# Norms behind the second feed-forward layer: the inverse deviations by GpSimd as a power, in place of ScalarE's square root and VectorE's reciprocal

## The reference, cut to what matters

```
h  = gelu(bi @ ffn_w1 + ffn_b1)
h  = gelu(h @ ffn_w2 + ffn_b2)
s  = x + h
H  = H + (s - mean(s)) * rsqrt(var(s) + 1e-5) * ln2_w + ln2_b
X  = (H - mean(H)) / sqrt(var(H) + 1e-5)
# then: per-channel and global extremes of X, from them scales and limits of an
# 8-bit quantization, quantized X and weights, a product, gelu, ...
```

## Time and profile before

| | us |
|---|---|
| median of three runs | 735.29 |
| lowest and highest of them | 730.75 and 736.48 |
| the profiled execution, its own time | 732.9 |
| its span in the profile | 730.9 |

### The profile page before, as it was taken

The page is one execution under the profiler, slowest core; times in us unless marked ns, Lnnn a source line. Parts: engine busy times, 40 slices in busy tenths (PEclk is TensorE's granted clock), DMA queues, the critical chain, the costliest instruction groups (busy, mean ns, idle before and its releaser), DMA issues.

```text
span 730.9 us, 13424 instructions
## 1 busy us (share of the span) xinstructions
PE 633.8 (87%) x4912; PEld 566.1 (77%) x4912; DVE 490.0 (67%) x1269; ACT 383.2 (52%) x875; POOL 277.1 (38%) x292
## 2 busy tenths in 40 slices
PE   3759898899899556568999999989999999999993
PEld 3659775569898432357888888979999999999993
DVE  3668688674604877657777785488587768677761
ACT  1349876873433466455665643442255656556540
POOL 5340525344301415042323353001244756666633
PEclk9959999999999756679999999999999999999997
DMA  6600000215000580300000110103095876768733
GB/s 181 120 1 5 1 1 1 98 50 147 1 0 1 148 150 0 120 0 5 4 4 4 25 72 2 48 1 120 19 320 153 250 234 198 261 177 254 200 95 69
DMA packets 27585, 64.67 MB, mean 88 GB/s; under 512 B 5951, under 2 KB 19152, under 8 KB 25184
## 3 DMA queue, kind: packets, MB, share of 16 engines
q0 software_dynamic: 12640, 46.90, 21.8%
q1 hardware_dynamic: 13116, 16.04, 8.3%
q10 hardware_dynamic: 1764, 0.88, 0.5%
HBM read 58.55 MB, written 5.74 MB: 88 GB/s over the span
## 4 chain that ended last, share of the span: by engine, by line
PE 46%; DVE 6%; issue 2%; ACT 2%; POOL 1%; DMA 0%; POOLq 0%; DVEq 0%; ACTq 0%
PE bank L1949 11%; PE bank L1909 4%; PE bank L1912 4%; PE bank L1913 4%; PE bank L1910 4%; PE bank L1911 4%; PE bank L1818 2%; PE bank L1754 2%; PE bank L1797 2%; DVE amx L2559 1%; PE bank L1774 1%; PE bank L1804 1%; PE bank L1716 1%; PE bank L1780 1%; DVE big L2565 1%
## 5 line engine op out<-in xcount | busy, mean ns | idle before, releaser
L2655 DVE TENSOR_SCALAR big<-bank 128x256 f32<-128x256 f32 (+1 forms) x126 | 52.3, 415 | 52.9 <-PE bank L1913 52.6
L1328 ACT ACTIVATE big<-bank 128x256 f32<-128x256 f32 (+1 forms) x126 | 47.5, 379 | 48.9 <-PE bank L1913 48.9
L811 POOL TENSOR_TENSOR big<-big,arc 128x423 f32<-128x423 f32 (+1 forms) x48 | 37.8, 814 | 73.6 <-DVE arc L2579 73.6
L837 POOL DMA_INDIRECT total<-big,goal x32 | 54.1, 1692 | 23.9 <-issue 17.5
L1909 PE MATMUL bank<-x_lead,w_lead 128*128 128x256 f32 x192 | 56.4, 294 | 0.0
L1912 PE MATMUL bank<-x_both,w_lead 128*128 128x256 f32 x192 | 54.4, 283 | 0.0
L1913 PE MATMUL bank<-x_both,w_rest 128*128 128x256 f32 x192 | 54.1, 282 | 0.0
L1911 PE MATMUL bank<-x_lead,w_rest 128*128 128x256 f32 x192 | 54.1, 282 | 0.0
L1910 PE MATMUL bank<-x_rest,w_lead 128*128 128x256 f32 x192 | 54.0, 281 | 0.0
L2666 DVE SCALAR_TENSOR_TENSOR big<-big 128x256 f32<-128x256 f32 (+1 forms) x126 | 50.4, 412 | 0.0
L844 POOL DMA_INDIRECT big<-x_rows,origin x32 | 34.0, 1061 | 33.9 <-DVE goal L2712 20.1
(11 more groups left out here) (542 smaller groups left out, 2022.9 us busy)
## 6 DMA issues: line engine op xcount, KB each, us to landing
big<-in_patches SPq DMA_DIRECT2D x2, 768.0 KB, 8.6
areg<-in_e_gate_up SPq DMA_DIRECT2D x1, 1536.0 KB, 6.5
shared_lead<-in_e_gate_up POOLq DMA_DIRECT2D x1, 1536.0 KB, 7.2
wreg<-in_ffn_w SPq DMA_DIRECT2D x1, 1152.0 KB
ffw_lead<-in_ffn_w POOLq DMA_DIRECT2D x1, 1152.0 KB, 7.8
out<-total SPq DMA_DIRECT2D x2, 423.0 KB
wreg<-in_in_w SPq DMA_DIRECT2D x2, 419.0 KB
wreg<-in_in_w SPq DMA_DIRECT2D x4, 209.5 KB
```

The costliest lines, as they stand in the source:

```text
L811: pool.tensor_tensor(o, o, arc[0:r, 18 * (b % 2) + 3 * g:18 * (b % 2) + 3 * g + q].unsqueeze(2).to_broadcast([r, q, L]), ALU.mult).then_in ...
L837: pool.indirect_dma_start(out=total, in_=YS[:, j % 2, q * D:(q + 1) * D], in_offset=None, out_offset=bass.IndirectOffsetOnAxis(ap=goal[:, ...
L1328: nc.scalar.activation(GS[:, n % 3, 0:w], bank[2 * (n % 2)][:, 0:w], ACT.Silu).then_inc(S["g_silu"], 1)
L2655: v.tensor_scalar(UM[:, n % 3, 0:w], bank[2 * (n % 2) + 1][:, 0:w], 10.0, -10.0, ALU.min, ALU.max).then_inc(S["u_clip"], 1)
```

## The change

GpSimd now computes, for each group, both inverse deviations: it adds 1e-5 to three variances (a `tensor_scalar` of 128x3), waits for that, and raises the sum to the power -0.5 (a `tensor_tensor` with a broadcast constant, operation `pow`). The first result goes to `rstd` as before, the second to `rstd2`. ScalarE's six square roots of this stage and VectorE's six reciprocals are gone. On VectorE the wait for the first inverse deviation moves behind the multiplication by the scale, in front of the instruction that reads it. On ScalarE the three `tokens_out` now stand behind all nine GELUs. The constant -0.5 is written once, while GpSimd has nothing else to do.

```diff
+            st.add(pool.memset(cst[:, 3:4], -0.5))
...
-            for t in range(6):
-                if t % 3 == 0:
-                    pool.wait_ge(S["rstd_ready"], t // 3 + 1)
-                pool.tensor_scalar(X[:, t, :], H[:, t, :], mv[:, t, 0:1], rstd[:, t:t + 1], ALU.subtract, ALU.mult).then_inc(ln_x, 1)
+            for g in range(3):
+                w = slice(3 * g, 3 * (g + 1))
+                pool.wait_ge(S["ln2_var"], 3 * (g + 1))
+                st.add(pool.tensor_scalar(std[:, w], mv[:, w, 1], EPS, None, ALU.add))
+                st.wait()
+                pool.tensor_tensor(rstd[:, w], std[:, w], cst[:, 3:4].to_broadcast([P, 3]), ALU.pow).then_inc(S["ln2_std"], 1)
+                pool.wait_ge(ln_var, TT + 3 * (g + 1))
+                st.add(pool.tensor_scalar(std[:, w], mv[:, w, 1], EPS, None, ALU.add))
+                st.wait()
+                pool.tensor_tensor(rstd2[:, w], std[:, w], cst[:, 3:4].to_broadcast([P, 3]), ALU.pow).then_inc(S["rstd_ready"], 1)
+                if g < 2:
+                    pool.wait_ge(S["rstd_ready"], g + 1)
+                    for t in range(3 * g, 3 * (g + 1)):
+                        pool.tensor_scalar(X[:, t, :], H[:, t, :], mv[:, t, 0:1], rstd2[:, t:t + 1], ALU.subtract, ALU.mult).then_inc(ln_x, 1)
...
             for t in range(TT):
                 act.wait_ge(S["f2_ready"], t + 1)
                 nc.scalar.activation(G2[0:rows(t), t, :], bank[4 + t % 4][0:rows(t), 0:D], ACT.Gelu).then_inc(S["f2_out"], 1)
-                if t % 3 == 2:
-                    deviations(t // 3, S["ln2_var"], t + 1, S["ln2_std"])
-                    if t == 5:
-                        tokens_out(0)
-                    if t == TT - 1:
-                        tokens_out(1)
-                    deviations(t // 3, ln_var, TT + t + 1, ln_std)
-            tokens_out(2)
+            for g in range(3):
+                tokens_out(g)
...
-                dve.wait_ge(ln_var, k * TT + 3 * (g + 1))
-                dve.wait_ge(ln_std, STD_BASE[k] + g + 1)
-                v.reciprocal(rstd[:, 3 * g:3 * (g + 1)], std[:, 3 * g:3 * (g + 1)]).then_inc(S["rstd_ready"], 1)
                 if g == 2:
...
-                dve.wait_ge(S["ln2_std"], g + 1)
-                st.add(v.reciprocal(rstd[:, 3 * g:3 * (g + 1)], std[:, 3 * g:3 * (g + 1)]))
                 for t in tiles3:
                     st.add(v.scalar_tensor_tensor(out=SS[:, t, :], in0=SS[:, t, :], scalar=mv[:, t, 0:1], in1=ln2w[:, :],
                                                   op0=ALU.subtract, op1=ALU.mult))
                 st.wait()
                 dve.wait_ge(S["x_kept"], TT + 1)
+                dve.wait_ge(S["ln2_std"], g + 1)
```

More of the change, by code:

```diff
@@ L421, in build @@
         LN_OUT = (2, 2, 2, 2)
-        STD_BASE = (0, 4, 7, 10)
+        STD_BASE = (0, 4, 4, 7)
         ON_DVE = (1, 4)
@@ L2304, in normalize @@
                     for t in tiles3:
-                        v.tensor_scalar(X[:, t, :], H[:, t, :], mv[:, t, 0:1], rstd[:, t:t + 1], ALU.subtract, ALU.mult).then_inc(ln_x, 1)
+                        v.tensor_scalar(X[:, t, :], H[:, t, :], mv[:, t, 0:1], rstd2[:, t:t + 1], ALU.subtract, ALU.mult).then_inc(ln_x, 1)
             def ranges(g):
```

## The result

| | before | changed |
|---|---|---|
| median of 8 runs, us | 732.77 | 739.87 |
| lowest and highest | 730.75, 736.48 | 736.06, 741.27 |
| span in the profile | 730.9 | 739.4 |

The ratio of changed to before is 1.0085, with a 95% interval of 1.0055 to 1.0115: slower by about 6.2 us, clear of noise. That is within the one per cent that the prediction called the same, though the interval reaches past it, and the median is inside the range of 733 to 743. The forecast of +3.9 us was too small by a third to a half. (The median before was 735.29 when the prediction was made, from its first three runs.)

The account below looks back on a forecast made before the run. The second layer's products, then the chain of small steps behind tile 8's last product, set the pace. 2.79 - 0.49 + 0.18 + 1.39 = +3.9 us on a mean of 734.2 gave 738, range 733 to 743.

Parts of the forecast that it names:

- The place: Behind tile 8's last product, a chain of small steps through group 2 to the statistics' square root sets the time.
- The copies behind the last GELU: ScalarE's copies of group 0 wait for tile 8's GELU, so VectorE starts group 2 late: 2.79 us lost.
- The table load: On ScalarE, a square-root table load now stands between the last cast and the statistics' root: 1.39 us lost.
- The larger figure, with a drain: The Trainium skill's 2.66 us per table switch, half a drain; it would add 1.4 us, sum about 5.3.
- GpSimd's path p: Hop from VectorE, addition, wait, power, hop back on GpSimd: 0.43 us plus a power of 0.40, so 0.83.
- the first norm: Group 2's first normalization: VectorE goes straight on to the scale multiplication, which covers GpSimd's work; 0.49 us saved.
- the second: Group 2's second normalization: from second variances to X, 0.65 us before, 0.83 now; 0.18 us lost.
- Price nothing: GpSimd's buffer clearing and nine transfers move some 7 us later behind group 2's second power; no cost, 1 us to spare.
- The dear power: Rival: a GpSimd power above 1.33 us delays group 0's X and tiles 7 and 8; 2.3 us gives some 744; 9%.
- First use: Rival: GpSimd's first power waits for its code, delaying group 0; a 5 us wait gives 741; 4%.
- The clock's rival: Rival: after the longer idle gap TensorE's clock returns later, so products take 2 us more, 740; 7%.
- The rival with no queueing: Rival: VectorE starts group 2 with the last GELU, despite instruction order; sum +0.3 us, 734.5; 3%.

Follow-up runs that it names:

- the gains of 0.8 and 1.2 us: Kernel before with only the first reciprocal moved behind the scale multiplication: 0.9978, again 0.9976; powers only for groups 0 and 1, copies early, clearing late: 0.9978.
- the run that hides it: Changed kernel plus one square root of a constant on ScalarE between the copies of groups 1 and 2, loading the table early: ratio 1.0081.
- its repeat: The changed kernel measured again, unaltered, on another run's chip, against the kernel before: median 738.66 us, ratio 1.0077.

## Why the prediction was right, and where it was not

- **The place was right.** The chain behind tile 8's product set the time; every edit that moved the root by 2 us or more moved the median in the same direction. Smaller moves the medians do not follow so well: the table load's 1.4 us did not show, and the gains of 0.8 and 1.2 us over the kernel before are not clear of noise.
- **The copies behind the last GELU: 2.79 predicted, 2.79 measured.** This is the largest term and its mechanism is shown from both sides, by putting them back (3.50, with VectorE's earlier readiness on top) and by delaying them in the kernel before (2.73).
- **The table load: 1.39 predicted, 1.41 measured.** The larger figure, with a drain, is refuted by the run that hides it.
- **GpSimd's path p was mis-sized: 0.83 predicted, 1.66 at the first norm and 1.33 at the second.** The power took 0.89 and not 0.40: that is between the stated ends of 0.17 and 1.20, but I put it near the price of an ordinary instruction, though no row had a power. The addition took 0.23 to 0.47 instead of 0.18, the 0.47 beside VectorE's multiplications, which the prediction did not look at. So the first norm gained nothing instead of 0.49, and the second lost 0.68 instead of 0.18. Together that is 1.0 us of the missing 1.7.
- **The term that was missing: the clearing.** "Price nothing" stood behind GpSimd's moved queue. The transfers were indeed free (the last two landed in 7.8 us instead of 15.7, and GpSimd used them no later than TensorE allowed), but the clearing at its head moved beside VectorE's X and held it for 0.67 us, the rest of the missing 1.7. I had looked at who waits for it, and not at what runs beside it.
- **The rivals.** The dear power did not come: with 0.89 us, group 0's X was ready at 235.34 + 3.00 = 238.34 against TensorE's 238.99. First use did not come: the first power took 0.91, the later ones 0.88 to 0.89. The clock's rival was half there, as pieces of both signs that leave +0.3 us in the changed kernel at the end of the attention, and -0.3 in its repeat. The rival with no queueing is out by the 3.50 us wait.
- **The range held partly by its width.** The prediction's sum ran from 3.6 to 5.3 us, and the stage took 5.54: outside it, since the clearing had no term. The range of 733 to 743 caught the median all the same, for it also allowed for the spread of the base and for the rivals.

The measured differences add up to 2.79 - 0.05 + 0.04 + 0.01 + 0.68 + 0.67 - 0.01 + 1.41 = 5.54, and the ratio's interval of 4.0 to 8.4 us holds it.

## What to carry to other kernels

When a wait leaves an engine, look at everything that was placed by it: here the copies moved behind three GELUs, and that cost more than both norms. Take a new kind of instruction at its own measured price, and where no row has one, give the upper bound as much weight as the lower. And of an instruction that is moved, ask also what it will run beside.

## What the runs showed of the hardware

- A power on GpSimd costs about 0.4 us and 0.16 us for each element of a partition (0.91, 1.33, 2.27 and 4.17 us for 3, 6, 12 and 24), where a multiplication of 24 takes 0.24.
- A table load on ScalarE costs 1.28 us and breaks the overlap of its neighbours, 1.42 in all; no further drain appeared.
- A clearing of 128x1128 two-byte elements by GpSimd held a VectorE instruction that reads one tensor (X, 0.37 us) for 1.07 us, and left the multiplications that read two (0.39 to 0.41 us) as they were.
- The other way round, these multiplications went with a slower addition on GpSimd: 0.46 to 0.48 us instead of 0.23, ending 0.1 us behind the multiplication that had begun just ahead of it.
- VectorE's additions beside GpSimd's X took up to 0.40 us instead of 0.34, and its batch statistics lost nothing.
